# Four graph layers on one core: the step of the gated recurrence in another order

## The chip, the cores and the metric

The kernel runs on one core of a Trainium2 chip. The metric is device microseconds of one execution. Before the change three runs took 805.19, 805.92 and 806.97 us (median 805.92). The five engines of the core each follow their own list of instructions and meet by semaphores: TensorE (PE in the rows; its weight loads are PEld), VectorE (DVE), ScalarE (ACT), GpSimd (POOL), and SyncE (SP), which issues the DMAs.

## The reference, cut to what matters

64 graphs of 128 nodes with 128 features go through four graph layers, each a residual on a layer norm. The first is a recurrence of five steps with a gated cell, and it is here that the change is:

```python
h = relu(layernorm(x))                       # 64 x 128 x 128
for l in range(5):
    m   = h @ weight[l]
    agg = einsum('bij,bid->bjd', A, m)       # A = adjacency != 0
    gi, gh = agg @ w_ih.T + b_ih, h @ w_hh.T + b_hh
    r = sigmoid(i_r + h_r); z = sigmoid(i_z + h_z)
    n = tanh(i_n + r * h_n)
    h = (1 - z) * n + z * h
x = x + h * mask
```

The second layer mixes a degree-normed aggregate with a linear part by a gate and an elu. The third works on the first 25 nodes in five overlapping groups with two normed convolutions each, weighted by a softmax. The fourth is one normed convolution with a relu.

## The kernel before, in words

The graphs go in 4 rounds of 16. A round has four quads of 4 graphs, so that a quad's state is one tile of 128 features by 512 columns. A step of the recurrence is one layer of one quad: 20 steps a round, 80 in all, numbered n. A quad comes up again four steps later. The weights of message and input gate are folded into one matrix per layer before the loop. Each of the three gate products is split into a high and a low half: three matmuls of 128x512 from the state (`state_product`, L408) and three from the aggregate (`message_product`, L411). The banks in PSUM are H_BANK (the state's part of the candidate), R_BANK, Z_BANK, I_BANK (the message's part of the candidate), TG (the turned state, and then the aggregate), and A, B, C for the other layers.

Layers two to four of a round run beside the recurrence of the next round. Their work is written out in advance by slots: step n has two, an even one 2n and an odd one 2n + 1, and constants at the top of the file (TURN1, LINEAR1, SUPPORT, CONV2 and so on) say at which slot a piece is due, counted from the start of the round. Each engine has a function `beside(slot)` that runs what is due on it, and the place of that call in the engine's step sets the order. The order is by program text alone; an engine takes its instructions in that order, and stops at a wait.

The step before, by engine:

- TensorE (L643 to L671): state product into H_BANK (which needs ScalarE's read of the last one), state product into R_BANK (which needs VectorE's `rh` of the last step), wait for ScalarE's read of H_BANK, even work, turn of the next step's state (`turn_h`, L390), wait for the low half of the aggregate, message product into R_BANK, state and message products into Z_BANK, message product into I_BANK (which needs the last new state, since that reads I_BANK), odd work, aggregate of the next step (`aggregate`, L399).
- ScalarE (L858 to L872): high half of the aggregate (`g_hi`, L860), read of H_BANK with its bias (L862, semaphore hb_ready), even work, read of the turned state (L855), tanh of R_BANK (L867), tanh of Z_BANK (L869), odd work, tanh of I_BANK (L872).
- VectorE: difference of the last step (L1295), low half of the aggregate (`g_lo`, L1301), new state of the last step (L1283, L1287, and its high half, L1290), even work, the product with r (L1307), its sum with the message's part (L1310), odd work.
- GpSimd: low half of the last step's new state (`low_half`, L915), even work, odd work. The low half is not made in the last layer of a round.

Pieces of the work beside that are named below: on TensorE the turn of the final state for layer two (L444), the turn of the normed rows and their sum over the adjacency (L456, L464), the linear parts (L478 to L490), the turn of the 25-node zone (L504), the support and the two convolutions of layer three (L517, L528, L540, L551), the turn back (L562), layer four (L573, L578, L580, L593), adjacency and block turns (L344, L375) and the turn of the next round's first rows (L362). On ScalarE, the layer norm's rows (L685), `first_h` (L694), the linear parts of layer two (L733, L735) and its exponential (L740, L744). On VectorE, statistics (L998, L1006), `l1_difference` (L1154) and the copy of the second support (L1188). On GpSimd `power` (L896 to L901), which makes the scale and shift of a layer norm for ScalarE.

Of the kernel before, what the change touches and what calls it, by code (L numbers as in the profile page):

```python
# [23 lines left out]
TURN_OUT, STATS1, AGGR1, NORM1, TURN1, LINEAR1, GATE1, EXP1, FINISH1 = -4, -4, -3, -2, 0, 1, 2, 3, 4  # L24
STATS2, NORM2, TURN2, PACK_EARLY, PACK_LATE = 6, 7, 8, 11, 15
# [10 lines left out]
def graph_stack(nc, x, adj, nodemask, conv_w, w_ih, w_hh, b_ih, b_hh, theta, W_h, W_t, b_t,  # L36
# [26 lines left out]
    with ctx:  # L63
# [271 lines left out]
        def _(pe):  # L335
# [42 lines left out]
            def turn_h(n):  # L378

                r, layer, q = n // STEPS, n % STEPS // QUADS, n % QUADS  # L380
                if layer == 0:
                    pe.wait_ge(sem["hx_ready"], r * QUADS + q + 1)
                    src = hx[q]
                else:
                    pe.wait_ge(sem["h_new"], n - QUADS + 1)
                    src = h[q]
                if n:
                    pe.wait_ge(sem["g_lo_ready"], n)
                for j in range(QUAD):
                    last = nc.tensor.transpose(TG[:, j * 128:(j + 1) * 128], src[:, j * 128:(j + 1) * 128], ident[:])  # L390
                last.then_inc(sem["h_turned"], 1)
# [16 lines left out]
            def state_product(dst, gate, q, stop=False):  # L408
                return split_matmul(dst, whh_hi[:, gate, :], whh_lo[:, gate, :], h_hi[q][:], h_lo[q][:], True, stop)

            def message_product(dst, gate, layer, start=False):  # L411
                c = slice(gate * 128, (gate + 1) * 128)
                return split_matmul(dst, wc_hi[:, layer, c], wc_lo[:, layer, c], g_hi[:], g_lo[:], start, True)
# [183 lines left out]
            def beside(slot):  # L597
                for r, q in due(slot, 1, TURN_OUT):
                    turn_out(r, q)
                for r, q in due(slot, 1, TURN2):  # L600
                    turn_zone(r, q)
                for r, k, at in second_conv(slot):
                    l2_conv2(r, k, at)
                for r, q in due(slot, 1, BACK):
                    turn_back(r, q)
                for r, q in due(slot, 1, AGGREGATE3):
                    l3_aggregate(r, q)
                for r, q in due(slot, 1, TURN1):
                    turn_and_sum(r, q)
                for r, q in due(slot, 1, LINEAR1):  # L610
                    l1_linear(r, q)
                for r, k in tile_at(slot, 2):
                    l2_support2(r, k)
                for r, k in tile_at(slot, 1):
                    l2_hidden(r, k)
                for r, k in tile_at(slot, 0):
                    l2_support(r, k)
                for r, q in due(slot, 1, TURN3):
                    turn_last_norm(r, q)
                for r, q in due(slot, 1, LINEAR3):  # L620
                    l3_linear(r, q)
                for r, q in due(slot, 0, TURN_ADJ, pace=1):
                    turn_adjacency(r, q)
                for r, q in due(slot, -1, TURN0):
                    turn_first_norm(r, q)
                for half in range(2):
                    for r, _ in due(slot, 0, TURN_BLOCKS[half], units=1):
                        turn_blocks(r, half)

            def h_bank_free(n):  # L630

                for r, q in due(2 * (n - 1), 1, TURN_OUT):
                    pe.wait_ge(sem["l1_x"], r * QUADS + q + 1)
                for r, q in due(2 * (n - 1), 1, TURN2):
                    pe.wait_ge(sem["zone_ready"], r * QUADS + q + 1)
                for r, k, at in second_conv(2 * (n - 1)):
                    pe.wait_ge(sem["l2_conv2_read"], r * NT + k + 1)
                for r, q in due(2 * (n - 1), 1, BACK):
                    pe.wait_ge(sem["l2_out"], r * QUADS + q + 1)
# [3 lines left out]
            for n in range(ALL):  # L643
                r, layer, q = n // STEPS, n % STEPS // QUADS, n % QUADS
                if layer == 0:
                    pe.wait_ge(sem["hx_lo"], r * QUADS + q + 1)
                else:
                    pe.wait_ge(sem["h_lo_new"], r * SPLITS + n % STEPS - QUADS + 1)
                if n:
                    pe.wait_ge(sem["hb_ready"], n)  # L650
                    h_bank_free(n)
                state_product(H_BANK, 2, q, True).then_inc(sem["gates_h"], 1)
                if n:
                    pe.wait_ge(sem["rh_ready"], n)
                state_product(R_BANK, 0, q)
                pe.wait_ge(sem["hb_ready"], n + 1)
                beside(2 * n)
                if n + 1 < ALL:
                    turn_h(n + 1)
                pe.wait_ge(sem["g_lo_ready"], n + 1)  # L660
                message_product(R_BANK, 0, layer).then_inc(sem["gates_r"], 1)
                if n:
                    pe.wait_ge(sem["z_ready"], n)
                state_product(Z_BANK, 1, q)
                message_product(Z_BANK, 1, layer).then_inc(sem["gates_z"], 1)
                if n:
                    pe.wait_ge(sem["h_new"], n)
                message_product(I_BANK, 2, layer, True).then_inc(sem["gates_n"], 1)
                beside(2 * n + 1)
                if n + 1 < ALL:  # L670
                    aggregate(n + 1)  # L671
# [6 lines left out]
        def _(act):  # L678
# [174 lines left out]
            def turned_h(n):  # L853
                act.wait_ge(sem["h_turned"], n + 1)
                nc.scalar.activation(hn[:], quad(TG[:, :]), ACT.Copy).then_inc(sem["hn_ready"], 1)  # L855

            turned_h(0)
            for n in range(ALL):  # L858
                act.wait_ge(sem["g_made"], n + 1)
                nc.scalar.activation(g_hi[:], TG[:], ACT.Copy).then_inc(sem["g_hi_ready"], 1)  # L860
                act.wait_ge(sem["gates_h"], n + 1)
                nc.scalar.activation(rh[:], H_BANK[:], ACT.Identity, bias=bhh[:, 2:3]).then_inc(sem["hb_ready"], 1)  # L862
                beside(2 * n)
                if n + 1 < ALL:
                    turned_h(n + 1)
                act.wait_ge(sem["gates_r"], n + 1)
                nc.scalar.activation(R_BANK[:], R_BANK[:], ACT.Tanh, bias=brz[:, 0:1], scale=0.5).then_inc(sem["r_ready"], 1)  # L867
                act.wait_ge(sem["gates_z"], n + 1)
                nc.scalar.activation(gz[n % 2][:], Z_BANK[:], ACT.Tanh, bias=brz[:, 1:2], scale=0.5).then_inc(sem["z_ready"], 1)  # L869
                beside(2 * n + 1)  # L870
                act.wait_ge(sem["pre_ready"], n + 1)
                nc.scalar.activation(I_BANK[:], I_BANK[:], ACT.Tanh, bias=bih[:, 2:3]).then_inc(sem["n_ready"], 1)  # L872
            for n in range(ALL, ALL + TAIL_STEPS):
                beside(2 * n)
                beside(2 * n + 1)
# [3 lines left out]
        def _(pool):  # L879
# [104 lines left out]
            for q in range(QUADS):  # L984
                first_low_half(0, q)
            for n in range(ALL + TAIL_STEPS):
                if n and n <= ALL and (n - 1) % STEPS < SPLITS:
                    low_half(n - 1)
                beside(2 * n)
                beside(2 * n + 1)  # L990


        @block.vector
        def _(dve):
# [299 lines left out]
                dve.wait_ge(sem["n_ready"], n + 1)  # L1294
                nc.vector.tensor_tensor(hd[:], (h if layer else hx)[q][:], I_BANK[:], ALU.subtract).then_inc(sem["hd_ready"], 1)  # L1295

            for n in range(ALL):
                if n:
                    difference(n - 1)
                dve.wait_ge(sem["g_hi_ready"], n + 1)  # L1300
                nc.vector.tensor_tensor(g_lo[:], TG[:], g_hi[:].bitcast(f32), ALU.subtract).then_inc(sem["g_lo_ready"], 1)  # L1301
                if n:
                    new_state(n - 1)
                beside(2 * n)
                dve.wait_ge(sem["hb_ready"], n + 1)
                dve.wait_ge(sem["r_ready"], n + 1)
                nc.vector.scalar_tensor_tensor(rh[:], R_BANK[:], 1.0, rh[:], ALU.add, ALU.mult).then_inc(sem["rh_ready"], 1)  # L1307
                dve.wait_ge(sem["rh_ready"], n + 1)
                dve.wait_ge(sem["gates_n"], n + 1)
                nc.vector.scalar_tensor_tensor(I_BANK[:], rh[:], 0.5, I_BANK[:], ALU.mult, ALU.add).then_inc(sem["pre_ready"], 1)  # L1310
                beside(2 * n + 1)
            difference(ALL - 1)
            new_state(ALL - 1)
            for n in range(ALL, ALL + TAIL_STEPS):
                beside(2 * n)
                beside(2 * n + 1)
# [23 lines left out]
```

## Time and profile before

| | |
|---|---|
| runs | 805.19, 805.92, 806.97 us; median 805.92 |
| profiled execution | 805.15 us, span 803.4 us |
| busy share of the span | PE 86%, PEld 71%, DVE 74%, ACT 65%, POOL 37% |
| mean granted TensorE clock | 0.97 |
| DMA | 21.08 MB, 26 GB/s |
| chain that ended last | PE 48%, ACT 22%, DVE 21%, issue 5% |

The first recurrent step starts 29.14 us into the span, after loads and the folding of the weights; the last one begins at 707.15, and what follows is the tail of the last round's layers two to four. A share of busy time is a mean over all of this. TensorE's matmuls overlap: one of 128x512 is shown with some 0.39 us, while the next starts 0.23 us after it.

### The profile page before, as it was taken

The numbers are of one execution on the slowest core, as the hardware profiler recorded it, in microseconds if no ns is written. First come the engines' busy times: TensorE is split into PE (matmuls) and PEld (weight loads), VectorE is DVE, ScalarE is ACT, GpSimd is POOL, SyncE is SP. The second block draws the span as 40 slices with busy tenths as digits, with TensorE's granted clock in tenths as the row PEclk, the third lists the DMA queues.
The fourth block names the chain that finished last, engine by engine and source line by source line (L and its number), as shares of the span: only waits on it lengthen the run. The fifth ranks groups of instructions, "written<-read, shape, count | busy, mean of one in ns | idle before, by whom it ended". The sixth has DMA issues, their size and how long they took to land.

```text
span 803.4 us, 12366 instructions
## 1 busy us (share of the span) xinstructions
PE 691.0 (86%) x4091; PEld 574.1 (71%) x4091; DVE 598.2 (74%) x1461; ACT 521.7 (65%) x1083; POOL 300.5 (37%) x423
## 2 busy tenths in 40 slices
PE   3888879999889998989989898989989998986665
PEld 2567667788777777868767777768767777776544
DVE  4677986788877886798887886797886896696233
ACT  4455757577667777657667777667766667666433
POOL 4212423553333443453143443463233234452320
PEclk9899989999999999999999999999999999999779
DMA  6600002100000020400000020110000000210001
GB/s 148 177 11 1 2 0 56 54 1 4 4 5 2 1 55 2 131 27 2 5 7 1 1 56 9 59 40 1 6 5 1 1 1 2 65 40 6 6 1 53
DMA packets 47623, 21.08 MB, mean 26 GB/s; under 512 B 9032, under 2 KB 47560, under 8 KB 47560
## 3 DMA queue, kind: packets, MB, share of 16 engines
q1 hardware_dynamic: 47560, 20.29, 9.3%
q8 instruction: 34, 0.56, 0.3%
q14 instruction: 29, 0.24, 0.1%
HBM read 15.27 MB, written 4.19 MB: 24 GB/s over the span
## 4 chain that ended last, share of the span: by engine, by line
PE 48%; ACT 22%; DVE 21%; issue 5%; POOL 2%; DMA 1%; DVEq 0%; SPq 0%; POOLq 0%; ACTq 0%
PE bank L404 7%; PE bank L406 7%; PE bank L405 7%; ACT bank L872 4%; PE bank L390 4%; ACT rh L862 4%; ACT g_hi L860 3%; DVE g_lo L1301 2%; ACT xn L685 2%; DVE bank L1310 2%; DVE hd L1295 2%; PE bank L593 2%; PE bank L540 2%; PE bank L528 2%; PE bank L580 2%
## 5 line engine op out<-in xcount | busy, mean ns | idle before, releaser
L915 POOL TENSOR_TENSOR h_lo<-h,h_hi 128x512 fp32r<-128x512 f32 x64 | 83.7, 1308 | 299.3 <-DVE h_hi L1290 299.3
L404 PE MATMUL bank<-h_hi,whh_hi 128*128 128x512 f32 x240 | 103.2, 430 | 4.6 <-DVE rh L1307 4.6
L404 PE MATMUL bank<-g_hi,wc_hi 128*128 128x512 f32 x240 | 103.1, 429 | 0.0
L405 PE MATMUL bank<-g_hi,wc_lo 128*128 128x512 f32 x240 | 95.8, 399 | 0.0
L406 PE MATMUL bank<-g_lo,wc_hi 128*128 128x512 f32 x240 | 95.7, 399 | 0.0
L405 PE MATMUL bank<-h_hi,whh_lo 128*128 128x512 f32 x240 | 95.2, 397 | 0.0
L406 PE MATMUL bank<-h_lo,whh_hi 128*128 128x512 f32 x240 | 95.2, 397 | 0.0
L399 PE MATMUL bank<-edge,hn 128*128 128x128 f32 x640 | 84.7, 275 | 0.8 <-ACT hn L855 0.8
L869 ACT ACTIVATE gz<-bank,brz 128x512 f32<-128x512 f32 x80 | 55.0, 688 | 45.1 <-PE bank L406 43.0
L399 PEld LDWEIGHTS bank<-edge,hn 128*128 128x128 f32 x640 | 80.8, 192 | 4.2 <-issue 1.0
L1307 DVE SCALAR_TENSOR_TENSOR rh<-bank,rh 128x512 f32<-128x512 f32 x80 | 54.9, 686 | 34.8 <-ACT bank L867 34.8
L1295 DVE TENSOR_TENSOR hd<-h,bank 128x512 f32<-128x512 f32 x64 | 43.8, 685 | 49.0 <-ACT bank L872 48.8
L1310 DVE SCALAR_TENSOR_TENSOR bank<-rh,bank 128x512 f32<-128x512 f32 x80 | 55.7, 696 | 25.1 <-PE bank L406 22.7
L896 POOL TENSOR_TENSOR var_eps<-mv,eps_ln 128x4 f32<-128x4 f32 (+1 forms) x64 | 21.5, 335 | 137.3 <-DVE mv L1006 122.5
L872 ACT ACTIVATE bank<-bank,bih 128x512 f32<-128x512 f32 x80 | 52.2, 653 | 28.5 <-DVE bank L1310 28.4
L685 ACT ACTIVATE xn<-x_res,shift,rstd 128x128 f32<-128x128 f32 x128 | 55.5, 483 | 12.9 <-POOL shift L901 12.9
L899 POOL TENSOR_TENSOR rstd<-var_eps,neg_half 128x4 f32<-128x4 f32 (+1 forms) x64 | 61.5, 961 | 5.0
L855 ACT ACTIVATE hn<-bank 128x512 f32<-128x512 f32 x80 | 47.5, 594 | 22.2 <-PE bank L390 22.2
L1283 DVE SCALAR_TENSOR_TENSOR zd<-gz,hd 128x512 f32<-128x512 f32 x80 | 58.8, 735 | 0.0
L1301 DVE TENSOR_TENSOR g_lo<-bank,g_hi 128x512 fp32r<-128x512 f32 x80 | 54.6, 683 | 3.3 <-ACT g_hi L860 3.3
L1287 DVE SCALAR_TENSOR_TENSOR h<-zd,bank 128x512 f32<-128x512 f32 x80 | 54.9, 687 | 2.8
L867 ACT ACTIVATE bank<-bank,brz 128x512 f32<-128x512 f32 x80 | 52.8, 660 | 5.8 <-PE bank L406 1.6
(167 smaller groups left out, 1630.0 us busy)
## 6 DMA issues: line engine op xcount, KB each, us to landing
x_in<-in_x SPq DMA_DIRECT2D x8, 512.0 KB, 5.5
adj_in<-in_adj SPq DMA_DIRECT2D x8, 512.0 KB, 4.8
x_res<-in_x SPq DMA_DIRECT2D x16, 256.0 KB, 2.8
out_x<-x_res SPq DMA_DIRECT2D x16, 256.0 KB, 2.3
xz<-x_res SPq DMA_DIRECT2D x16, 50.0 KB
w_sb<-in_L_gnn_W SPq DMA_DIRECT2D x1, 640.0 KB, 5.2
w_sb<-in_L_gnn_W SPq DMA_DIRECT2D x5, 128.0 KB, 5.1
rows<-in_adj SPq DMA_DIRECT2D x32, 0.6 KB
```

What stands on the lines that cost most here:

```text
L399: last = nc.tensor.matmul(TG[:, j * 128:(j + 1) * 128], hn[:, j, :], edge[:, q * QUAD + j, :], start=True, stop=True)
L404: nc.tensor.matmul(dst[:], w_hi, m_hi, start=start, stop=False)
L405: nc.tensor.matmul(dst[:], w_lo, m_hi, start=False, stop=False)
L406: return nc.tensor.matmul(dst[:], w_hi, m_lo, start=False, stop=stop)
L685: last = nc.scalar.activation(dst[:, b, :], src[:, b, :], ACT.Relu, bias=shift[i][:, b:b + 1], scale=rstd[i][:, b:b + 1])
L872: nc.scalar.activation(I_BANK[:], I_BANK[:], ACT.Tanh, bias=bih[:, 2:3]).then_inc(sem["n_ready"], 1)
L899: nc.gpsimd.tensor_tensor(rstd[i][0:p, c], var_eps[i][0:p, c], neg_half[0:p, c], ALU.pow).then_inc(sem[f"ln{L}_pow"], 1)
L915: nc.gpsimd.tensor_tensor(h_lo[q][:], h[q][:], h_hi[q][:].bitcast(f32), ALU.subtract).then_inc(sem["h_lo_new"], 1)
L1283: nc.vector.scalar_tensor_tensor(zd[:], gz[n % 2][:], 1.0, hd[:], ALU.add, ALU.mult).then_inc(sem["zd_ready"], 1)
L1295: nc.vector.tensor_tensor(hd[:], (h if layer else hx)[q][:], I_BANK[:], ALU.subtract).then_inc(sem["hd_ready"], 1)
L1301: nc.vector.tensor_tensor(g_lo[:], TG[:], g_hi[:].bitcast(f32), ALU.subtract).then_inc(sem["g_lo_ready"], 1)
L1310: nc.vector.scalar_tensor_tensor(I_BANK[:], rh[:], 0.5, I_BANK[:], ALU.mult, ALU.add).then_inc(sem["pre_ready"], 1)
```

## The change

The step's order is changed on four engines. TensorE does all three state products first, then waits for the low half of the aggregate and does the turn, then the even work, then all three message products, the odd work and the next aggregate. It waits for ScalarE's read of H_BANK ahead of the even work only if that work writes H_BANK. ScalarE makes the high half of the next aggregate right after the tanh of Z_BANK, ahead of the tanh of I_BANK, reads the turned state ahead of the even work, and has its odd work after the tanh of I_BANK. VectorE makes the low half of the next aggregate, the difference and the new state within the same step, and has its odd work after them. GpSimd makes the low half of the state between its even and its odd work of the same step.

```diff
+            def h_bank_taken(slot):
+                return due(slot, 1, TURN_OUT) or due(slot, 1, TURN2) or second_conv(slot) or due(slot, 1, BACK)
...
                 state_product(R_BANK, 0, q)
-                pe.wait_ge(sem["hb_ready"], n + 1)
-                beside(2 * n)
-                if n + 1 < ALL:
-                    turn_h(n + 1)
-                pe.wait_ge(sem["g_lo_ready"], n + 1)
-                message_product(R_BANK, 0, layer).then_inc(sem["gates_r"], 1)
                 if n:
                     pe.wait_ge(sem["z_ready"], n)
                 state_product(Z_BANK, 1, q)
+                pe.wait_ge(sem["g_lo_ready"], n + 1)
+                if n + 1 < ALL:
+                    turn_h(n + 1)
+                if h_bank_taken(2 * n):
+                    pe.wait_ge(sem["hb_ready"], n + 1)
+                beside(2 * n)
+                message_product(R_BANK, 0, layer).then_inc(sem["gates_r"], 1)
                 message_product(Z_BANK, 1, layer).then_inc(sem["gates_z"], 1)
...
-            turned_h(0)
-            for n in range(ALL):
+            def aggregate_hi(n):
                 act.wait_ge(sem["g_made"], n + 1)
                 nc.scalar.activation(g_hi[:], TG[:], ACT.Copy).then_inc(sem["g_hi_ready"], 1)
+
+            turned_h(0)
+            aggregate_hi(0)
+            for n in range(ALL):
                 act.wait_ge(sem["gates_h"], n + 1)
                 nc.scalar.activation(rh[:], H_BANK[:], ACT.Identity, bias=bhh[:, 2:3]).then_inc(sem["hb_ready"], 1)
-                beside(2 * n)
                 if n + 1 < ALL:
                     turned_h(n + 1)
+                beside(2 * n)
...
-                beside(2 * n + 1)
+                if n + 1 < ALL:
+                    aggregate_hi(n + 1)
                 act.wait_ge(sem["pre_ready"], n + 1)
                 nc.scalar.activation(I_BANK[:], I_BANK[:], ACT.Tanh, bias=bih[:, 2:3]).then_inc(sem["n_ready"], 1)
+                beside(2 * n + 1)
...
-                if n and n <= ALL and (n - 1) % STEPS < SPLITS:
-                    low_half(n - 1)
                 beside(2 * n)
+                if n < ALL and n % STEPS < SPLITS:
+                    low_half(n)
                 beside(2 * n + 1)
...
-            for n in range(ALL):
-                if n:
-                    difference(n - 1)
+            def aggregate_lo(n):
                 dve.wait_ge(sem["g_hi_ready"], n + 1)
                 nc.vector.tensor_tensor(g_lo[:], TG[:], g_hi[:].bitcast(f32), ALU.subtract).then_inc(sem["g_lo_ready"], 1)
-                if n:
-                    new_state(n - 1)
+
+            aggregate_lo(0)
+            for n in range(ALL):
                 beside(2 * n)
...
                 nc.vector.scalar_tensor_tensor(I_BANK[:], rh[:], 0.5, I_BANK[:], ALU.mult, ALU.add).then_inc(sem["pre_ready"], 1)
+                if n + 1 < ALL:
+                    aggregate_lo(n + 1)
+                difference(n)
+                new_state(n)
                 beside(2 * n + 1)
-            difference(ALL - 1)
-            new_state(ALL - 1)
```

## Rows read from the trace of the kernel before

**Rows 1.** Stretches: 20, 20, 20, 19 steps, then step 79 and tail: busy us (x instructions), PEclk, DMA.
```profile
29.14:168.73 139.59, 123.38 (x653) 98.75 (x651) 107.43 (x243) 86.99 (x156) 46.60 (x51) 0.98 0.14 37
168.73:351.59 182.86, 166.30 (x1021) 140.24 (x1019) 146.31 (x355) 128.02 (x270) 74.69 (x105) 0.99 0.09 25
351.59:534.21 182.62, 164.88 (x1020) 139.06 (x1019) 147.46 (x357) 128.07 (x270) 74.70 (x104) 1.00 0.07 20
534.21:707.15 172.94, 158.36 (x970) 133.72 (x969) 134.34 (x303) 115.86 (x240) 61.32 (x79) 0.99 0.04 11
707.15:803.40 96.25, 64.61 (x393) 52.93 (x391) 46.71 (x152) 49.51 (x122) 30.43 (x56) 0.85 0.07 19
```
**Rows 2.** Who waited for whom on TensorE: total us, times, longest us.
```profile
PE bank L390 <- DVE g_lo L1301: 11.3, 17, 1.9
...
PE bank L504 <- ACT rh L862: 10.3, 12, 1.9
```
**Rows 3.** Timeline of a light step: start us, us, engine line, [idle before <-releaser].
```profile
67.59 1.05 PE L399 MATMUL bank<-edge,hn 128*128 128x128 f32 x8
...
68.40 0.48 PE L404 MATMUL bank<-h_hi,whh_hi 128*128 128x512 f32 x1
68.59 0.66 ACT L872 ACTIVATE bank<-bank,bih 128x512 f32<-128x512 f32 x1 [0.81 <-DVE bank L1310]
...
69.17 0.59 ACT L860 ACTIVATE g_hi<-bank 128x512 fp32r<-128x512 f32 x1
...
69.66 0.39 PE L406 MATMUL bank<-h_lo,whh_hi 128*128 128x512 f32 x1
...
70.72 0.63 PE L390 MATMUL bank<-ident,h 128*128 128x128 f32 x4 [0.68 <-DVE g_lo L1301]
...
74.80 0.48 PE L404 MATMUL bank<-h_hi,whh_hi 128*128 128x512 f32 x1
```
**Rows 4.** Timeline of step 46, the seventh of the third round: VectorE, TensorE.
```profile
413.91 0.28 DVE L1188 COPY sup<-bank 100x128 f32<-100x128 f32 x1
...
414.73 0.69 DVE L1295 TENSOR_TENSOR hd<-h,bank 128x512 f32<-128x512 f32 x1 [0.54 <-ACT bank L872]
...
416.08 0.43 PE L551 MATMUL bank<-normT,sup 100*128 100x100 f32 x2
...
417.37 0.43 DVE L1290 CAST h_hi<-h 128x512 fp32r<-128x512 f32 x1
```
**Rows 5.** Timeline of ScalarE's odd work in slot 5 of the third round.
```profile
382.92 0.60 ACT L733 ACTIVATE gate_th<-bank 128x512 f32<-128x512 f32 x1 [1.13 <-PE bank L481]
...
385.49 0.86 ACT L685 ACTIVATE xn<-x_res,shift,rstd 128x128 f32<-128x128 f32 x2
386.26 0.63 ACT L872 ACTIVATE bank<-bank,bih 128x512 f32<-128x512 f32 x1
```
**Rows 6.** Stretches of the third round: steps 0 to 3, 4 and 5, 6 to 11, 12 to 19.
```profile
351.59:396.38 44.79, 41.00 (x279) 35.92 (x278) 36.68 (x88) 31.24 (x59) 16.46 (x23) 1.00 0.01 3
396.38:413.71 17.33, 13.86 (x78) 10.95 (x76) 15.13 (x27) 11.44 (x24) 6.17 (x10) 1.00 0.01 4
413.71:465.63 51.92, 47.75 (x289) 39.93 (x288) 42.02 (x119) 39.35 (x98) 20.67 (x31) 1.00 0.01 2
465.63:534.21 68.58, 62.28 (x384) 52.25 (x383) 53.63 (x127) 46.04 (x92) 31.40 (x40) 1.00 0.17 48
```
**Rows 7.** Timeline of GpSimd in steps 53 and 54.
```profile
477.56 1.29 POOL L915 TENSOR_TENSOR h_lo<-h,h_hi 128x512 fp32r<-128x512 f32 x1 [1.81 <-DVE h_hi L1290]
...
482.35 0.20 POOL L896 TENSOR_TENSOR var_eps<-mv,eps_ln 128x4 f32<-128x4 f32 x1
...
483.86 0.20 POOL L901 TENSOR_TENSOR shift<-neg_mean,rstd 128x4 f32<-128x4 f32 x1
```
**Rows 8.** Stretches: step 5 of the second round, and the same step of the third.
```profile
219.51:231.21 11.70, 9.02 (x44) 7.02 (x43) 9.30 (x16) 6.56 (x14) 3.44 (x7) 0.85 0.03 9
403.56:413.71 10.15, 7.47 (x45) 5.89 (x43) 8.84 (x15) 6.57 (x14) 3.45 (x7) 1.00 0.03 7
```

## The prediction, written before the changed kernel ran

> **What bounds the kernel now.** I read the stretches by round first [rows 1]. The recurrence runs in four rounds of 20 steps (139.59, 182.86, 182.62 us, and 172.94 for 19 steps of the last); the last 96.25 us are its twentieth step and a tail with no recurrence. In the first round little beside it is due, in the other three the layers of the round before are. TensorE is busy for 123.38 of 139.59 us and for about nine tenths of the later rounds: what can be won is its pauses, 16.21 us in the first round and 16.56, 17.74 and 14.58 in the others.
>
> The waits of TensorE say where they are [rows 2]: the turn of the next state (L390) stands before the low half of the aggregate (L1301), and the work beside (L504 and its like) before ScalarE's read of H_BANK (L862). A light step shows the loop [rows 3]: 6.40 us from one first state product to the next. ScalarE does the tanh of I_BANK (68.59), then g_hi (69.17), VectorE g_lo, and only then the turn starts at 70.72. The sixth state product began near 69.66 and takes 0.23 us to the next start, so about 0.83 us of each light step is a pause.
>
> **The clock of a step after the change.** I count from H, the start of the first state product. The aggregate is seen done at H+0.24 (67.59+1.05 against 68.40) [rows 3]. g_hi now comes first: +0.28 to +0.88. The tanh of I_BANK starts at +0.80 and ends at +1.46, if VectorE's sum for it is there. The difference starts at +1.52 behind g_lo; three operations of 0.69 make h_new +3.65, and with the cast of 0.43 VectorE is free at +4.05 [rows 4]. TensorE does nine state products until +2.20 and the turn until +2.64; g_lo (done +1.6) no longer stops it. ScalarE's wait for the aggregate now has the tanh, the odd work and the H_BANK read queued behind it; since VectorE's sum is mostly there by H+0.16, the tanh comes 0.6 later than in the light step of rows 3, and the difference and new_state with it. Call E the start of its even work, Pe and Po its even and odd work (0.11 us for one of the 128x128 passes, of which eight take 1.05, and 0.23 for a 128x512). Then the step is E + Pe + Po + 3.05: nine message products, the aggregate, and 0.05 of switching. Without work beside it is 5.6.
>
> **First round: gain.** Eight steps at 5.6 (44.8); five with adjacency and block turns at 8.05, 6.4, 6.5, 6.1, 6.1; the seven in which VectorE is last at 6.9, 6.1, 6.45, 7.0, 11.95, 6.2, 6.75. There VectorE's own loop is 4.6 us plus all its work beside, because the odd part no longer stands under the tanh. Sum 129.3 against 139.59: -10.3. If g_lo were late after all the gain is 0, if every pause went it is 16.2.
>
> **Later rounds: three things move behind the new state, and TensorE's even work needs them.** Bounds of each: 0 if a longer wait covers it, and the figure given.
>
> 1. ScalarE's odd work now follows the tanh, so it stands ahead of its H_BANK read of the next step. That read ends at 1.36 + odd work + 0.69. In 16 of 20 steps H_BANK is taken and E = 2.11 + odd work. Before, odd work ended ahead of the tanh: in slot 5 (five groups from 382.92 to 386.35) the tanh waits behind it until 386.26 [rows 5]. That wait goes; the next even work inherits it. In steps 2 and 3 of a round no H_BANK is used, but the turn of L456 needs the normalised rows that are last in the 3.11 us: E = 4.53. Its sums (L464) wait further for VectorE's l1_difference, 4.05 + 1.13 + 0.06 = 5.24. Steps 0 to 3: 13.1 (VectorE comes late into the first), 12.1, 12.1, 12.1 = 49.4 against 44.79 [rows 6]: +4.6. Steps 4 and 5 (odd work 2.73 and 2.03): 8.47 + 9.91 = 18.4 against 17.33: +1.1.
>
> 2. The second convolution of an odd tile (L551) reads the copy of sup2 (L1188), which VectorE makes in the slot just before. Now that slot comes after new_state: before, the copy was at 413.91, ahead of the difference at 414.73, and L551 at 416.08 had it long since [rows 4]. After: 4.05 + 0.28 + 0.06 = 4.39. Six steps in a row (6 to 11) start that matmul at 4.39 (the last, where VectorE is 1.7 late, at 5.29), with 1.09, 1.17, 1.07, 1.50, 1.16, 0.73 of even work after it and 1.29, 0.86, 1.30, 1.29, 0.44, 0.43 of odd: 9.82 + 9.48 + 9.8 + 10.23 + 9.04 + 9.5 = 57.9 against 51.92 [rows 6]: +5.9.
>
> 3. On GpSimd low_half (1.29) now stands ahead of the odd work, and its wait for h_hi holds the power chain behind it (482.35 to 484.06, 1.71) [rows 7]. Steps 12 to 15 of a round have that chain in an odd slot and ScalarE's normalisation (0.87) with first_h (0.6) in the next even slot, ahead of the tanh of R_BANK. After: 4.2 + 1.3 + 1.75 = 7.3, the tanh of R_BANK not before 8.8; the block turns (L375) need first_h as well. Steps 12 to 19: 7.85, 10.0, 10.07, 11.07, 8.68, 8.9, 7.15, 6.77 = 70.5 against 68.58 [rows 6]: +1.9. The last four gain from the shorter loop; 13 to 15 lose 4.
>
> Together +13.5 for rounds two and three; the fourth has no first_h and I take +12.5. What goes: the pauses at L862, of 16.56 to 17.74 us in all per round; what is late next: VectorE's new state.
>
> H_BANK's condition takes the wait away only in steps 2, 3, 16, 17; worth nothing in the first two. The loads on SP wait for l1_out, stored and norms, which move by less than a step: 0. The tail's program is the same: 0. The last difference and new_state move into the loop: 0.
>
> **Sum.** 805.15 us is the profiled execution (its span 803.4 and 1.75 around it), 0.77 under the median of 805.92. -10.3 + 13.5 + 13.5 + 12.5 = +29.2: 834.4, or 835 for the median.
>
> **TensorE's clock.** The same step 5 took 11.70 us in the second round at a mean granted clock of 0.85 and 10.15 in the third at 1.00, after like pauses [rows 8]: a pause of about 2 us is sometimes followed by matmuls at 1.2 instead of 2.4 GHz, and costs 1.55 then. The Trainium skill, "TensorE: Matmul & The Clock Gate" (HAM oscillation), says that pauses between groups of matmuls throttle the clock again and that the cost is paid at every group. By that rule each new pause would count; of the two like pauses of rows 8 one agrees with it and one does not. I take it as a rival.
>
> **Rivals.**
> - *Engine-bound (12%).* The new order drops the pauses in heavy rounds too, because the three results come in time. For: the loop through g_hi, g_lo and the turn is shorter by the 0.83 us of rows 3. Against: VectorE works in order, and L1188 and L1154 stand behind new_state. All pauses gone: -16.56 -17.74 -14.58 -10.3 = -59, 746; with VectorE last in a quarter of the steps about two thirds of it, 770.
> - *Evened out (8%).* Only the conv2 wait (5.9) bites; odd work of ScalarE fits under the nine products. 3 x 5.9 - 10.3 - 3 x 2 = +1: 807.
> - *Clock falls (15%).* About eight pauses of 1.4 us or more per heavy round follow from points 1 to 3 (steps 0 to 5, 13 to 15); if most bring the low clock, 24 x 1.55 = 37: up to 872, with half of them 853.
> - *Slower by the three waits (65%):* 835. Its own range 816 to 856: each heavy step is right to about 0.35 us, 60 of them in one direction are 20.
>
> The point at which the sign turns: heavy rounds must lose less than 3.4 us each, a quarter of what I count.
>
> **Range and chances.** 803 to 862 leaves out the engine-bound case, half of the evened-out one's lower part and the end of the clock case. A measurement here tells 0.2% (1.6 us) from no change. Faster: the first rival and a quarter of the second, 14%. Same: 4%. Slower: 82%.
>
> **What would show it.** Right: light steps of 5.6 us with no wait of L390 on g_lo; L551 waiting for L1188 in six steps of each heavy round; L456 waiting longer for xn and L444, L504, L562 longer for L862; L375 waiting for first_h; ScalarE's xn (L685) waiting for GpSimd's shift; round one near 129 us, two and three near 196. Wrong: heavy rounds under 183 us, or L551 starting right behind the turn; or light steps still at 6.4, which says that g_lo still ends the wait.

## The result and the profile after

The changed kernel took 848.61 us in the median of four runs (846.56 to 850.43), the kernel before 805.91 beside it; the ratio is 1.0528 [1.0501 to 1.0555], slower. The profiled execution is 848.84 us (span 846.9 us, mean granted clock 0.95) against 805.15. The forecast of 835 has the sign, and falls short by 13.6. I read the trace as I had read the one of before: first the stretches by round and the tail, which answer to [rows 1] with the same columns.

```profile
29.14:157.87 128.73, 122.21 (x652) 99.58 (x651) 108.04 (x238) 83.61 (x150) 42.70 (x47) 0.97 0.16 41
157.87:355.85 197.98, 172.39 (x1018) 145.41 (x1018) 145.90 (x357) 126.51 (x269) 74.25 (x105) 0.97 0.08 22
355.85:553.29 197.44, 171.35 (x1017) 144.43 (x1018) 145.79 (x357) 126.39 (x269) 73.78 (x104) 0.97 0.07 18
553.29:740.93 187.64, 162.54 (x968) 137.52 (x968) 135.20 (x305) 117.14 (x245) 64.90 (x82) 0.97 0.04 10
740.93:846.90 105.97, 72.20 (x393) 59.61 (x391) 47.97 (x153) 50.35 (x122) 29.72 (x56) 0.77 0.07 20
```

The first round gains 10.86 us, the heavy rounds lose 15.12, 14.82 and 14.70, and the last step with the tail loses 9.72: +43.5 in all. TensorE's busy time in the third round grew as well, from 164.88 to 171.35 us, for the same matmuls at a clock of 0.97 instead of 1.00. The waits of TensorE answer to [rows 2].

```profile
PE bank L456 <- ACT xn L689: 18.4, 9, 4.3
PE bank L404 <- DVE rh L1315: 16.3, 15, 3.7
PE bank L551 <- DVE sup L1197: 13.1, 16, 1.4
PE bank L504 <- ACT rh L869: 11.5, 12, 1.9
...
PE bank L562 <- ACT rh L869: 9.8, 10, 1.9
...
PE bank L375 <- ACT hx L698: 5.6, 2, 2.8
```

The first line of before, the turn L390 that waits for g_lo, is gone. New in its place stand the normalised rows and the copy of the second support, and with two long waits `first_h` (L375): they are late because of work that now stands behind the tanh, the new state or low_half. The second line is VectorE coming late to the product with r, which TensorE's next state product needs (16.3 us, of it 3.66 in step 11; 4.6 before). The waits for the read of H_BANK are not new, and in all they are shorter: TensorE waited 48.2 us for it before and 32.2 now. Two of their lines before, beside that of L504 in [rows 2]:

```profile
PE bank L562 <- ACT rh L862: 8.7, 9, 1.5
PE bank L444 <- ACT rh L862: 6.9, 8, 1.6
```

The light step that answers to [rows 3] (start, us, engine line) shows the gain.

```profile
63.92 0.48 PE L404 MATMUL bank<-h_hi,whh_hi 128*128 128x512 f32 x1
64.20 0.60 ACT L863 ACTIVATE g_hi<-bank 128x512 fp32r<-128x512 f32 x1 [0.91 <-PE bank L399]
...
66.11 0.60 PE L390 MATMUL bank<-ident,h 128*128 128x128 f32 x4
...
69.45 0.48 PE L404 MATMUL bank<-h_hi,whh_hi 128*128 128x512 f32 x1
```

It takes 5.53 us (6.40 before); g_hi starts at H+0.28, and the turn follows the ninth state product without a pause. The third round by stages answers to [rows 6].

```profile
355.85:406.36 50.51, 43.38 (x276) 37.46 (x277) 35.93 (x88) 31.23 (x60) 20.31 (x26) 0.97 0.03 8
406.36:424.62 18.26, 15.10 (x77) 12.38 (x76) 15.22 (x28) 12.51 (x25) 6.11 (x10) 0.91 0.02 6
424.62:480.96 56.34, 48.73 (x289) 40.71 (x288) 40.74 (x118) 38.56 (x96) 20.66 (x31) 1.00 0.00 1
480.96:553.29 72.33, 64.14 (x384) 53.88 (x383) 53.89 (x124) 44.09 (x88) 26.70 (x37) 0.98 0.15 41
```

Predicted were 49.4, 18.4, 57.9 and 70.5; the sums agree within 1.3 us, but in part because errors cancel (below). One step of each kind follows. Step 42, for the first point: ScalarE comes to the normalised rows at 384.17 behind four pieces of odd work, TensorE's turn L456 waits for them until H+4.44 (H is 380.65; predicted 4.53), and L464 for VectorE's l1_difference until H+5.29 (predicted 5.24).

```profile
384.17 0.86 ACT L689 ACTIVATE xn<-x_res,shift,rstd 128x128 f32<-128x128 f32 x2
384.68 1.12 DVE L1163 SCALAR_TENSOR_TENSOR diff<-bank,norm,hetS 128x128 f32<-128x128 f32 x4
385.09 0.65 PE L456 MATMUL bank<-ident,xn 128*128 128x128 f32 x4 [1.65 <-ACT xn L689]
385.94 1.13 PE L464 MATMUL bank<-adjT,xn 128*128 128x128 f32 x8 [0.20 <-DVE diff L1163]
```

Step 46 (H 424.62), for the second, answers to [rows 4]: the copy of the second support comes right behind the new state's cast, and L551 starts at H+4.36 (predicted 4.39).

```profile
428.30 0.43 DVE L1299 CAST h_hi<-h 128x512 fp32r<-128x512 f32 x1
428.64 0.28 DVE L1197 COPY sup<-bank 100x128 f32<-100x128 f32 x1
428.98 0.47 PE L551 MATMUL bank<-normT,sup 100*128 100x100 f32 x2 [1.09 <-DVE sup L1197]
```

Step 53 (H 488.56), for the third, answers to [rows 7]: low_half ahead of the power chain, then ScalarE, then TensorE's block turn, which waits 2.80 us; before, the step took 7.08 us, now 11.80.

```profile
493.68 1.29 POOL L924 TENSOR_TENSOR h_lo<-h,h_hi 128x512 fp32r<-128x512 f32 x1 [7.26 <-DVE h_hi L1299]
496.45 0.20 POOL L910 TENSOR_TENSOR shift<-neg_mean,rstd 128x4 f32<-128x4 f32 x1
496.68 0.88 ACT L689 ACTIVATE xn<-x_res,shift,rstd 128x128 f32<-128x128 f32 x2 [4.13 <-POOL shift L910]
497.46 0.57 ACT L698 ACTIVATE hx<-bank 128x512 f32<-128x512 f32 x1
498.09 0.86 PE L375 MATMUL bank<-ident,blocks 100*100 100x100 f32 x4 [2.80 <-ACT hx L698]
```

Last the entry of the tail, step 79 (H 740.93), which I had costed at nothing. VectorE makes the statistics that the power chain needs behind the new state of step 78; ScalarE's first half of the normalised rows then stands ahead of the last tanh of R_BANK and the second half behind the tanh of I_BANK, and the turn L456 starts at H+11.07. Before it started at H+6.31.

```profile
747.27 0.20 POOL L910 TENSOR_TENSOR shift<-neg_mean,rstd 128x4 f32<-128x4 f32 x1
747.51 0.88 ACT L689 ACTIVATE xn<-x_res,shift,rstd 128x128 f32<-128x128 f32 x2 [4.05 <-POOL shift L910]
748.29 0.64 ACT L874 ACTIVATE bank<-bank,brz 128x512 f32<-128x512 f32 x1
751.08 0.87 ACT L689 ACTIVATE xn<-x_res,shift,rstd 128x128 f32<-128x128 f32 x2
752.00 1.11 PE L456 MATMUL bank<-ident,xn 128*128 128x128 f32 x4 [4.30 <-ACT xn L689]
```

### The profile page after: what moved, and what is told of

Its sections match the earlier page's. It is cut to its first block, busy times and chain, and to the rows that moved or that the text cites. A ratio compares the mean times of both kernels' runs of the same rounds, so it can differ in the third digit from the quotient of the medians.

```text
span 846.9 us, 12359 instructions
## 1 busy us (share of the span) xinstructions
PE 714.3 (84%) x4091; PEld 596.2 (70%) x4091; DVE 598.6 (71%) x1461; ACT 517.3 (61%) x1083; POOL 298.1 (35%) x423
## 4 chain that ended last, share of the span: by engine, by line
PE 49%; DVE 27%; ACT 14%; issue 5%; POOL 4%; DMA 1%; DVEq 0%; SPq 0%; POOLq 0%; ACTq 0%
PE bank L399 7%; PE bank L404 6%; PE bank L406 6%; PE bank L405 6%; DVE zd L1292 4%; DVE hd L1304 4%; DVE h L1296 4%; ACT g_hi L863 3%; DVE g_lo L1308 3%; PE bank L540 2%; PE bank L517 2%; PE bank L464 2%; PE bank L528 2%; ACT xn L689 2%; ACT bank L880 2%
## 5 line engine op out<-in xcount | busy, mean ns | idle before, releaser
L924 POOL TENSOR_TENSOR h_lo<-h,h_hi 128x512 fp32r<-128x512 f32 x64 | 81.8, 1278 | 394.4 <-DVE h_hi L1299 394.4
L863 ACT ACTIVATE g_hi<-bank 128x512 fp32r<-128x512 f32 x80 | 47.9, 598 | 119.2 <-PE bank L399 119.2
L404 PE MATMUL bank<-h_hi,whh_hi 128*128 128x512 f32 x240 | 105.6, 440 | 17.8 <-DVE rh L1315 16.3
L404 PE MATMUL bank<-g_hi,wc_hi 128*128 128x512 f32 x240 | 106.1, 442 | 0.7 <-DVE h L1296 0.3
L406 PE MATMUL bank<-g_lo,wc_hi 128*128 128x512 f32 x240 | 97.6, 407 | 0.0
L399 PE MATMUL bank<-edge,hn 128*128 128x128 f32 x640 | 87.5, 281 | 0.8 <-ACT hn L859 0.8
L399 PEld LDWEIGHTS bank<-edge,hn 128*128 128x128 f32 x640 | 83.9, 198 | 4.7 <-issue 1.0
L404 PEld LDWEIGHTS bank<-h_hi,whh_hi 128*128 128x128 f32 x240 | 46.3, 193 | 32.9 <-DVE rh L1315 24.4
L874 ACT ACTIVATE bank<-bank,brz 128x512 f32<-128x512 f32 x80 | 52.2, 653 | 12.6 <-PE bank L406 10.4
L1292 DVE SCALAR_TENSOR_TENSOR zd<-gz,hd 128x512 f32<-128x512 f32 x80 | 56.5, 706 | 2.8
```

The costliest lines, as they stand in the source:

```text
L399: last = nc.tensor.matmul(TG[:, j * 128:(j + 1) * 128], hn[:, j, :], edge[:, q * QUAD + j, :], start=True, stop=True)
L404: nc.tensor.matmul(dst[:], w_hi, m_hi, start=start, stop=False)
L406: return nc.tensor.matmul(dst[:], w_hi, m_lo, start=False, stop=stop)
L924: nc.gpsimd.tensor_tensor(h_lo[q][:], h[q][:], h_hi[q][:].bitcast(f32), ALU.subtract).then_inc(sem["h_lo_new"], 1)
L1292: nc.vector.scalar_tensor_tensor(zd[:], gz[n % 2][:], 1.0, hd[:], ALU.add, ALU.mult).then_inc(sem["zd_ready"], 1)
```

## The experiments

The kernel before took 811.28 us in the median of the first group of experiments (the first four), 806.78 in the second (the next four) and 810.91 in the third, where its single runs lay between 804.52 and 812.45; so ratios are compared, and step lengths from the profiles.

**One wait of TensorE taken away.** VectorE's copy of the second support ahead of the low half of the aggregate, its other odd work where the change put it:

```diff
+                copy_support2(2 * n + 1)
                 if n + 1 < ALL:
                     aggregate_lo(n + 1)
```

> The changed kernel, with VectorE's copy of the second support in odd slots (L1188 before the change) back between its sum for the tanh and the low half of the aggregate; nothing else moves. Theory (three waits): the second convolution in steps 6 to 11 of a heavy round starts after the H_BANK read at 3.0 to 3.7 us into the step instead of at 4.4 behind the copy; those six steps fall from 56.3 to about 52.2, three rounds give -12.6: about 836 us. Rival (VectorE's loop or the H_BANK read sets these steps anyway): 848, the wait only changes its name.

Measured 828.33 us, ratio 1.0233 [1.0174 to 1.0292]. In step 46 the wait of 1.09 us for the copy is gone, and L551 stands right behind the turns and a wait of 0.20 us for the read of H_BANK:

```profile
421.56 0.28 PE L504 MATMUL bank<-ident,xz 100*128 100x100 f32 x1 [0.20 <-ACT rh L869]
421.71 0.44 PE L551 MATMUL bank<-normT,sup 100*128 100x100 f32 x2
```

Steps 46 to 51 take 50.97 us instead of 56.34: the second point is real, and its price is 5.4 us in the second and in the third round and 7.5 in the fourth, 18 in all against the 12.6 that I had expected. The ratio fell by more, from 1.053 to 1.023, and the profiled execution, the slowest of the four, is only 14.3 us shorter than that of the changed kernel; what makes the difference is not shown.

**GpSimd's low_half behind the odd work.**

```diff
                 beside(2 * n)
+                beside(2 * n + 1)
                 if n < ALL and n % STEPS < SPLITS:
                     low_half(n)
-                beside(2 * n + 1)
```

> The changed kernel, with GpSimd's low half of the state after its odd work instead of before it. Theory: the norm's power chain runs 1.3 us earlier in steps 12 to 15 of a heavy round, ScalarE's rows and first_h with it, so step 13 falls by about 1.3 and the two after it by 0.5 each: -2.5 a round, about 841 us. The tail's entry stays, as steps 78 and 79 make no low half. Rival (GpSimd is off the path, the chain waits for VectorE's new state alone): 848.

Measured 832.2 us, ratio 1.0275 [1.023 to 1.0319]. Step 53 takes 10.39 us instead of 11.80, step 54 9.68 instead of 9.98, step 57 8.49 instead of 9.43: 2.65 us in the third round. More was saved than expected, and part of it is not the queue: step 53 ran at a mean clock of 0.94 instead of 0.89, and the tail took 100.98 us instead of 106.00 with the same late entry (11.08), at another clock. The same 112 or 113 matmuls, from the first turn of the zone (L504) to the first turn back (L562), in the changed kernel:

```profile
780.61:815.92 35.31, 25.81 (x113) 20.40 (x113) 8.92 (x28) 15.93 (x53) 8.53 (x16) 0.65 0.01 4
```

and with low_half last:

```profile
768.48:799.33 30.85, 20.39 (x112) 15.75 (x112) 8.92 (x28) 15.59 (x53) 8.55 (x16) 0.83 0.01 4
```

**ScalarE's odd work ahead of the halves again, nothing else.**

```diff
+                beside(2 * n + 1)
                 if n + 1 < ALL:
                     aggregate_hi(n + 1)
...
-                beside(2 * n + 1)
```

> The changed kernel, with ScalarE's odd work back ahead of the high half of the aggregate and the tanh of I_BANK. Theory: the H_BANK read and the normalised rows come in time again, but in steps 1 to 3 the sums still wait for VectorE's l1_difference and in steps 6 to 11 for its copy, and where ScalarE's odd work ends after the aggregate the high half comes up to 0.75 us later: 846 to 852 us. Rival (point 1 of the prediction as its numbers stand: ScalarE's odd work ahead of the H_BANK read is what costs 5.7 us a round): -17, about 831.

Measured 866.16 us, ratio 1.0692 [1.0652 to 1.0732]: outside every expectation, and slower than the whole change. Step 42 (here H 386.06) shows why: L456 no longer waits, but g_hi comes only at H+0.96, and with it g_lo, the new state and VectorE's odd work behind that, so L464 waits 2.47 us for the difference. The step takes 14.26 us at a mean clock of 0.88, against 12.08 at 1.00 in the changed kernel. The same step of the round before, 22, has the same wait of 2.47 us and took 12.72 at 1.00: the order costs 0.64 us there, and the other 1.54 go with the lower clock. Steps 46 and 48, too, ran at 0.86 and 0.85, and the clock is part of this loss.

```profile
387.02 0.58 ACT L863 ACTIVATE g_hi<-bank 128x512 fp32r<-128x512 f32 x1
...
390.73 1.12 DVE L1163 SCALAR_TENSOR_TENSOR diff<-bank,norm,hetS 128x128 f32<-128x128 f32 x4
392.00 1.13 PE L464 MATMUL bank<-adjT,xn 128*128 128x128 f32 x8 [2.47 <-DVE diff L1163]
```

The three points are not three prices that add up. Here an engine's odd work came onto the path where it stood behind something that is late.

**TensorE's new order alone, in the kernel before.** The other three engines are as they were.

> The kernel before, with TensorE's order of the change alone: three state products, turn, even work, three message products; the other engines as before. Theory: the Z state products leave the loop tanh - high half - low half - turn - messages, 0.7 us of a light step (6.40 to 5.7), and in heavy steps 0.7 less 0.25 for the low half that is ready later than the H_BANK read; no new wait on VectorE, ScalarE or GpSimd: 770 to 785 us, 778. Rival (the loss of the change comes from TensorE's order itself, the even work being late behind the turn): above 806.

Measured 780.39 us, ratio 0.9629 [0.9592 to 0.9666], faster than before. A light step takes 5.71 us, the rounds 130.55, 176.60, 176.76 and 166.74: TensorE's order gains in light and heavy rounds alike, and what made the change slow is what the other engines' order adds to it.

**The whole change run again** beside the next three:

> The changed kernel as it is, beside the kernel before on the chip of these runs, since the kernel before took 811 us where the first three edits ran and 806 elsewhere. Expected of every theory: a ratio near 1.053. If it is under 1.045 or over 1.06, part of what the edits showed belongs to the chip.

Measured 849.5 us, ratio 1.0531 [1.0488 to 1.0575].

**The change with the odd work of all three engines back ahead.** ScalarE as two experiments before, low_half last, and VectorE:

```diff
+                beside(2 * n + 1)
                 if n + 1 < ALL:
                     aggregate_lo(n + 1)
                 difference(n)
                 new_state(n)
-                beside(2 * n + 1)
```

> The changed kernel with the odd work of ScalarE, VectorE and GpSimd all back where it was (ahead of the high half, of the low half and of the state's low half); TensorE's order, the high half ahead of the tanh and the low half ahead of the difference stay. Theory (the three moves of odd work are the whole loss): no wait of L551 on the copy, none of L456 on late rows, the second layer's entry into the tail back at 6 us after the last step's start; light steps stay at 5.53; heavy rounds 172 to 178 us; ratio 0.95 to 0.965, at or a little under TensorE's order alone (0.963). Rival (the high half ahead of the tanh makes the new state late by itself): heavy rounds above 183, ratio above 0.98.

Measured 766.5 us, ratio 0.9492 [0.9434 to 0.955]: better than both kernels. The rounds take 127.81, 172.06, 172.31 and 162.06 us; the third of them, and the last step with the tail:

```profile
328.99:501.30 172.31, 162.90 (x1020) 139.26 (x1019) 149.66 (x357) 127.58 (x269) 76.24 (x104) 1.00 0.07 21
...
663.36:758.81 95.45, 63.36 (x393) 51.37 (x391) 47.25 (x152) 49.43 (x122) 30.67 (x56) 0.87 0.07 20
```

Light steps still take 5.53 us, so the halves, the difference and the new state within the step are kept; the heavy rounds are 25 us shorter than with the change. The place of the odd work, on the three engines together, is the whole loss. VectorE's alone was not tried.

**The same, but ScalarE's odd work, and of VectorE's the l1_difference, left where the change put them.**

> The changed kernel with VectorE's odd work back ahead of the low half, but for l1_difference, and GpSimd's low half last; ScalarE's odd work stays behind the tanh. Theory (waits 2 and 3 of the prediction go, wait 1 stays): steps 6 to 11 at 51 as with the copy alone, step 13 near 7.3 instead of 11.8, the tail's entry 4.8 us earlier, steps 1 to 3 still at 12.1; heavy rounds near 185, ratio 0.99 to 1.005. Rival (the waits overlap, ScalarE's odd work covers most of what waits 2 and 3 cost): ratio above 1.02.

Measured 803.44 us, ratio 0.9951 [0.9916 to 0.9986]. Rounds of 128.74, 184.03, 184.25 and 174.22 us: 12 a heavy round above the last kernel, and the entry of the tail 8.94 us against 6.37 (I had expected 6.3). Steps 41 to 43 are at 12.08 us as in the changed kernel. So this part of the order costs some 37 us when everything else is back, and the rest of VectorE's and GpSimd's odd work 13 to 14 a heavy round.

**The wait for H_BANK always**, as the kernel before has it:

```diff
-                if h_bank_taken(2 * n):
-                    pe.wait_ge(sem["hb_ready"], n + 1)
+                pe.wait_ge(sem["hb_ready"], n + 1)
```

> The changed kernel with TensorE's wait for the H_BANK read in every step again. Theory: only steps 2 and 3 of a heavy round can tell, where L456 would start at 5.2 instead of 4.5 us but its sums wait for l1_difference until 5.24 anyway: +0.4 each, +2.6 us in all; ratio within 0.005 of the changed kernel's. Rival (the condition is a good part of the change): light steps or the tail slower, +8 us or more.

Measured 854.99 us, ratio 1.0598 [1.0553 to 1.0644] beside 1.0531 for the changed kernel. The intervals overlap, the steps are clearer: 0.42 to 0.58 us more in steps 9, 12, 14 and 15, 0.8 in 36, 56 and 76, 0.44 in 37, 57 and 77, and 0.15 in 42. The theory had looked for it in steps 2 and 3 of a heavy round alone.

**Twelve turns more in a pause**, in the changed kernel: of the identity into A_BANK, in the second to fourth quad.

```diff
                 if q:
                     pe.wait_ge(sem["l1_het"], u)
+                    for i in range(12):
+                        nc.tensor.transpose(A_BANK[:, i % 4 * 128:(i % 4 + 1) * 128], ident[:], ident[:])
                 pe.wait_ge(sem["ln1_xn"], u + 1)
```

> The changed kernel with twelve more turns of 128x128 (of the identity, into A_BANK, about 1.3 us) on TensorE ahead of the wait for the normalised rows in the turn L456 of the second to fourth quad. They stand where TensorE paused 1.65 us and their result is overwritten. If the low granted clock of steps 23/24, 43/44 and 63/64 comes from these pauses: those pairs take 12.1 + 8.2 instead of 13.65 + 9.8, 3.15 less in each of three rounds, and the kernel takes about 9 us less than the changed kernel, ratio to the kernel before about 1.04. Rival, that the clock falls for another reason, or that the added turns only lengthen the steps: 1.053 or more, steps 41 to 43 at 12.1 or longer and the low clock still in 43 and 44.

Measured 844.06 us, ratio 1.0431 [1.039 to 1.0472]. The stretches of steps 42 to 45 in the changed kernel (after the five busy times the granted clock, the share of the DMAs and GB/s):

```profile
380.65:392.74 12.09, 10.24 (x71) 8.89 (x69) 8.39 (x19) 8.23 (x16) 3.76 (x5) 1.00 0.02 6
392.74:406.36 13.62, 11.78 (x70) 10.07 (x69) 8.46 (x17) 7.55 (x14) 3.02 (x5) 0.87 0.01 4
406.36:416.15 9.79, 7.87 (x36) 6.31 (x35) 8.38 (x17) 6.31 (x12) 3.04 (x5) 0.83 0.02 6
416.15:424.62 8.47, 7.24 (x44) 6.07 (x43) 6.85 (x11) 6.20 (x13) 3.07 (x5) 1.00 0.02 6
```

and steps 43 to 45 with the added turns:

```profile
393.72:405.80 12.08, 11.54 (x82) 10.18 (x81) 8.38 (x17) 7.57 (x14) 3.03 (x5) 1.00 0.02 6
405.80:414.00 8.20, 6.27 (x36) 5.10 (x35) 6.97 (x15) 6.32 (x12) 3.03 (x5) 1.00 0.00 1
414.00:424.72 10.72, 8.87 (x44) 7.16 (x43) 8.33 (x14) 6.32 (x13) 3.07 (x5) 0.84 0.03 10
```

Steps 43 and 44 come out as expected at the full clock, 3.13 us less; but the fall moves on to step 45, which gives 2.25 back, and steps 21, 41 and 61 are 0.7 longer. The turns left 0.34 us of the pause of 1.65. That they moved the fall is not shown. Here it went so in all three rounds, and in the two profiles of the changed kernel in none; but with low_half last and no turn added, steps 23 to 25 have the same pause of 1.65 us and took 12.07, 8.21 and 10.71 us at 1.00, 1.00 and 0.84. In the profiled execution, the slowest of its eight runs, nothing is left of the gain; the median is 4.5 us under that of the changed kernel, half of what I expected, and since the kernel before spread by 8 us here, I don't count on it.

**Only the last three steps with the odd work back**, on ScalarE and VectorE:

```diff
+                if n >= ALL - 3:
+                    beside(2 * n + 1)
                 if n + 1 < ALL:
                     aggregate_lo(n + 1)
...
+                if n < ALL - 3:
+                    beside(2 * n + 1)
```

> The changed kernel, but in steps 77 to 79 alone the odd work of ScalarE and VectorE stands ahead of the halves of the next aggregate, as it did before. If the late entry of the tail comes from the odd work of step 78: from the start of step 79 to the first turn L456 6.4 us instead of 11.07, and the kernel 4.7 us shorter, ratio about 1.047; about 1.042 if TensorE's clock in layer three of the tail also comes out high (30.9 us from the first L504 to the first L562 instead of 35.3). Rival, that the entry is late because step 79 itself is in the new order: entry about 11 and ratio 1.053.

Measured 840.86 us, ratio 1.0394 [1.0346 to 1.0443]. In step 79 (H 736.61) both halves of the normalised rows are done by the tanh of Z_BANK, and L456 starts at H+6.37:

```profile
740.13 0.88 ACT L689 ACTIVATE xn<-x_res,shift,rstd 128x128 f32<-128x128 f32 x2 [1.48 <-POOL shift L913]
...
742.05 0.87 ACT L689 ACTIVATE xn<-x_res,shift,rstd 128x128 f32<-128x128 f32 x2
742.98 0.66 PE L456 MATMUL bank<-ident,xn 128*128 128x128 f32 x4 [0.41 <-ACT xn L689]
```

The late entry of the tail is the odd work of the last steps: 4.70 us. The edit covers steps 77 to 79 together, but the kernel that leaves ScalarE's odd work behind the tanh tells them apart. Its step 79 (H 701.21) has the first half of the rows as early as here (H+3.51 against H+3.52) and the second behind the tanh of I_BANK, at H+8.03 against H+5.44:

```profile
709.24 0.86 ACT L689 ACTIVATE xn<-x_res,shift,rstd 128x128 f32<-128x128 f32 x2
```

Its entry is at 8.94. So 2.13 us are VectorE's odd work of step 78 with the statistics, and 2.57 ScalarE's odd work of step 79 itself: the rival of the expectation was right for a good half. The stretch from L504 to L562 stays long (35.17 us), so that part has another cause. Most of the rest goes with the clock in this profile, which fell in fewer steps than in the changed kernel's (11, 24 and 33 at 1.00, step 33 10.74 us instead of 11.80).

## Why the prediction was right in sign and short in size

**First round.** -10.86 against -10.3. The clock of a light step held point by point: g_hi at H+0.28, new state done at H+3.65, nothing of the turn's wait left. Step 11, priced at 11.95, took 13.07 at a mean clock of 0.74, little less than the 13.36 that it took before at the same clock; the other steps made up for it.

**Heavy rounds.** +15.1, +14.8 and +14.7 against +13.5, +13.5 and +12.5, by the three mechanisms named, but for one part of the first. The sizes of the third round, with steps grouped as in [rows 6]: +5.7 against +4.6, +0.9 against +1.1, +4.4 against +5.9, +3.7 against +1.9. Under this lies a second cause that I had set apart as a rival: steps 43, 44, 53 and their like ran at a low mean clock. At 1.00 they are shorter: step 43 by 1.55 (run with the added turns), steps 44 and 45 together by 0.90 (17.36 against 18.26, from the same steps of the second round, 24 and 25, in the last run; 44 gives 1.59, and 45 waits longer behind it), step 53 by 1.06 (step 33 of the last run), about 3.5 us a round. Without it the third round loses some 11.3 us, not the 13.5 that I counted. The part that failed is the later read of H_BANK in steps 4 and 5: at 1.00 the two take 17.36 us, the 17.33 of before, so that their +0.9 is the clock and not the read. Nor did the sign come that L444 would wait longer for it (4.5 us against 6.9). Single steps were off as well: steps 45 and 51 above all were priced too high (9.91 and 9.5 against 9.16 and 8.44 at 1.00), steps 53, 57 and 59 too low (10.0, 8.9 and 6.77 against 10.74, 9.43 and 7.49). So the term came out near through two errors of opposite sign, which is luck, and the clock rival was true in part beside the likeliest case, not instead of it. The two were no alternatives.

**The tail.** Here the step failed: "The tail's program is the same: 0." The program is the same, but its input is the odd work of steps 78 and 79, which the change moved like every other. Of the +9.72 us, 4.76 are the entry, by the third mechanism of the prediction (statistics, power chain, normalisation) one step further on, and by ScalarE's odd work behind the last tanh, shown by the last experiment and the one with VectorE's odd work back. The stretch from L504 to L562 has 4.4: 35.3 us at a clock of 0.65. Over the profiles of this case that stretch takes either 30.9 us (before, low_half last, odd work back) or 34.6 to 35.8, whether the entry is early or late; TensorE's order alone, with an early entry of 6.17, has 35.1. So it isn't the late entry, and what decides it is open.

**H_BANK's condition.** I had it "worth nothing in the first two" and looked at steps 2 and 3 alone. The steps named above show about 2.1 us in the first round and some 1.4 in a heavy one. There TensorE's even work leaves H_BANK alone: turns of the adjacency and of the next rows (L344, L362) in steps 12, 14 and 15, layer four's sums (L593) in 36 and 37, the turn L456 in 42, and nothing in step 9.

**The rivals.** "Engine-bound" expected that the pauses go in heavy rounds too, at 746 to 770 us. It is wrong for this change. The same order with the odd work back comes into its range with 766.5, though not all pauses are gone there: the third round takes 172.31 us with TensorE busy for 162.90. "Evened out" took ScalarE's odd work to fit under the nine products; left behind the tanh with the l1_difference, it cost some 37 us.

**The clock.** In steps 42 and 43 TensorE pauses alike ahead of L456 (1.65 us each), and only the second pause is followed by matmuls at the lower of the two levels, 1.2 instead of 2.4 GHz (step 43 has a mean of 0.87): message products that start 0.43 us apart where they start 0.23 apart in step 42. With the pause of step 43 filled the fall came two steps later, but elsewhere it came so without the filling. The Trainium skill, "TensorE: Matmul & The Clock Gate" (HAM oscillation), describes a kernel whose waits for DMA, longer than these pauses, throttle the clock again ahead of each group of matmuls. The trace agrees in kind and not in count: of these two like pauses one was paid for.

## What to carry to other kernels

When work is reordered in engines that take their instructions in order, price every instruction that ends up behind the moved one, and ask of each who reads it a step later and whether the last step has a reader in the part that "does not change". Try the parts of a reordering one by one: here one engine's new order alone was worth 4%, and the same order with the filler work of the other engines left ahead was worth 5%, while the whole change cost 5%. Prices of single moves did not add: undoing ScalarE's alone made it worse, undoing GpSimd's alone made it better, and undoing all three made it the fastest.

## What the runs showed of the hardware that I had not expected

The same pauses brought a fall of the clock in one profile and not in another. With the pause of step 43 filled, the fall left steps 43 and 44 (3.13 us) and came back in step 45 (2.25 us), and with low_half last the second round had it in step 25 without any filling. It also differs between profiled executions of almost the same work: steps 33 and 34 took 11.80 and 10.22 us in the changed kernel, and 10.74 and 9.91, at a clock of 1.00, in the one that differs from it only in its last three steps.
